# First loads cut and reordered, first layer norm in two parts of two tiles

## The reference, cut to what matters

```
x = x + attention0(layernorm(x))     # 3 heads, softmax over the first token axis, then mean over heads, fc
x = x + ffn0(layernorm(x))           # ternary-quantised weights
x = x + attention1(layernorm(x))     # 16 heads, causal
x = x + ffn1(layernorm(x))           # int8 product
layernorm(x) = (x - mean) / sqrt(var + 1e-5)
attention0: Q = x Wq[h].T, K = x Wk[h].T, V = x Wv[h].T
            scores = Q K.T / 16,  out = mean over h of softmax(scores) V,  then out @ fc_w.T + fc_b
```

## Time and profile before

| | us |
|---|---|
| median of three runs | 505.29 |
| the profiled execution | 505.88 |
| its span in the trace | 504.10 |
| PE busy | 482.8 (96%) |
| DVE busy | 378.2 (75%) |
| ACT busy | 295.4 (59%) |
| POOL busy | 282.5 (56%) |
| TensorE clock granted, mean | 0.991 |

### The profile page before, as it was taken

One profiled execution on the slowest core, in us unless ns is written; L12 is line 12 of the kernel. 1 busy time (PEld: TensorE's weight loads), 2 busy tenths in 40 slices (PEclk: granted clock), 3 DMA queues, 4 the chain that ended last, 5 costly groups with the idle time before them and its releaser, 6 DMA issues.

```text
span 504.1 us, 8912 instructions
## 1 busy us (share of the span) xinstructions
PE 482.8 (96%) x3020; PEld 429.8 (85%) x3020; DVE 378.2 (75%) x964; ACT 295.4 (59%) x694; POOL 282.5 (56%) x378
## 2 busy tenths in 40 slices
PE   8999999999999977899999999999999999999984
PEld 7888998899888856799888999899889989899972
DVE  2776776775746578788779888788878897667897
ACT  2355336535554645676667676667757766655663
POOL 1344244323665556786667786777767796511344
PEclk9999999999999999999999999999999999999996
DMA  9900000000010017564864764764765654100002
GB/s 278 380 22 2 1 0 1 0 1 1 24 42 1 0 46 184 159 187 109 213 182 127 195 181 114 210 179 122 202 178 149 177 170 131 36 1 1 0 2 83
DMA packets 54380, 51.58 MB, mean 102 GB/s; under 512 B 3520, under 2 KB 49728, under 8 KB 54336
## 3 DMA queue, kind: packets, MB, share of 16 engines
q1 hardware_dynamic: 53248, 49.98, 34.7%
q10 hardware_dynamic: 1088, 1.05, 0.6%
HBM read 32.92 MB, written 18.09 MB: 101 GB/s over the span
## 4 chain that ended last, share of the span: by engine, by line
PE 71%; DVE 13%; POOL 4%; issue 4%; DMA 3%; ACT 3%; SPq 1%; DVEq 0%; POOLq 0%; ACTq 0%
PE bank L405 19%; PE bank L407 18%; PE bank L406 18%; PE bank L700 3%; PE bank L698 3%; PE bank L699 3%; POOL HID_lo L1156 2%; DMA Wv_sb<-wv 2%; DVE BT L1535 2%; PE bank L628 1%; PE bank L627 1%; DVE SM L1516 1%; PE bank L709 1%; ACT E L906 1%; DMA turned_dram<-BT 1%
## 5 line engine op out<-in xcount | busy, mean ns | idle before, releaser
L1187 POOL TENSOR_TENSOR PT_lo<-MV,PT_hi 128x512 fp32r<-128x512 f32 (+1 forms) x104 | 91.5, 909 | 51.5 <-ACT PT_hi L998 51.1
L987 ACT ACTIVATE PR<-SM,nmax 128x128 f32<-128x128 f32 (+3 forms) x128 | 72.0, 563 | 62.6 <-DVE nmax L1516 62.1
L1132 POOL TENSOR_TENSOR E_lo<-E,E_hi 128x512 fp32r<-128x512 f32 x24 | 31.0, 1297 | 54.0 <-ACT E_hi L911 46.8
L1516 DVE CUSTOM_DVE_ANT_0 SM<-bank,causal 128x384 f32<-128x384 f32 (+3 forms) x102 | 54.0, 530 | 9.3 <-PE bank L700 6.4
L405 PE MATMUL bank<-XT_hi,W_hi 128*128 128x512 f32 x128 | 52.3, 409 | 5.2 <-DVE V_lo L1498 3.7
L998 ACT CAST PT_hi<-MV 128x512 fp32r<-128x512 f32 (+1 forms) x104 | 42.1, 453 | 19.6 <-DMA MV<-turned_dram 19.2
L1535 DVE STREAM_TRANSPOSE BT<-PR 128x128 f32<-128x128 f32 (+1 forms) x104 | 48.2, 492 | 5.6 <-POOL PR L1171 3.8
L407 PE MATMUL bank<-XT_hi,W_lo 128*128 128x512 f32 x128 | 50.5, 394 | 0.0
L406 PE MATMUL bank<-XT_lo,W_hi 128*128 128x512 f32 x128 | 50.2, 392 | 0.0
L406 PE MATMUL bank<-PT_lo,V_hi 128*128 128x128 f32 (+3 forms) x130 | 41.5, 319 | 0.0
L407 PE MATMUL bank<-PT_hi,V_lo 128*128 128x128 f32 (+3 forms) x130 | 41.5, 319 | 0.0
(11 more groups left out here) (189 smaller groups left out, 1602.6 us busy)
## 6 DMA issues: line engine op xcount, KB each, us to landing
MV<-turned_dram SPq DMA_DIRECT2D x104, 160.0 KB, 3.2
turned_dram<-BT SPq DMA_DIRECT2D x26, 384.0 KB, 2.9
stage<-pack SPq DMA_DIRECT2D x32, 256.0 KB, 3.9
turned_dram<-BT SPq DMA_DIRECT2D x26, 256.0 KB, 3.3
X<-x SPq DMA_DIRECT2D x2, 512.0 KB, 8.9
wraw<-wupT SPq DMA_DIRECT2D x1, 1024.0 KB, 9.6
wraw<-wgateT SPq DMA_DIRECT2D x1, 1024.0 KB, 11.5
wraw<-wdownT SPq DMA_DIRECT2D x1, 1024.0 KB, 13.7
```

The source lines that it names most:

```text
L987: act.activation(PR[:, c, 0:(c + 1) * P], SM[:, c % 2, 0:(c + 1) * P], ACT.Exp, bias=nmax1[:, c:c + 1], scale=-1.0, accum_out=sum1[:, c:c ...
L1132: pool.tensor_tensor(E0_lo[:, m, :], E0[:, m, :], E0_hi[:, m, :], ALU.subtract).then_inc(e0_lo, 1)
L1187: pool.tensor_tensor(by_quad(PT_lo[w % 2], c), moved_part(w, c), by_quad(PT_hi[w % 2], c), ALU.subtract).then_inc(mv_lo, 1)
L1516: dve.tensor_tensor_reduce(SM[:, c % 2, 0:n], s_bank(w, c)[:, 0:n], mask, 1.0, HIGHEST, ALU.add, ALU.min, nmax1[:, c:c + 1]).then_inc(s_ma ...
```

## The change

It does five things.

1. Wk and Wq of head 0 are loaded in two halves of 128 KB (128 rows each), each pair with a semaphore of its own (`ld_first`). Use 0 on PE goes over the half (d) outside and over the columns (e) inside, so that its first two products need the first halves only.
2. On SP, Wv of head 0 stands ahead of x; x of sequence 0 comes in two loads of two tiles (`ld_x0`). Wv of heads 1 and 2 goes to ACT's queue, behind fcT, which keeps its place.
3. The first statistics, the addition of epsilon and the power are done for tiles 0 and 1, then for tiles 2 and 3 (`first_var`, `first_rstd`), and normalising waits for each part by itself.
4. On PE, tiles 0 and 1 are transposed in front of the first half of use 5, tiles 2 and 3 in front of its second half.
5. `project_y` waits for XT_lo of one half of the columns at a time.

The diff, cut to its core:

```diff
         def _(sp):
-            for h in range(H0):
+            for k in range(KD):
+                sp.dma_start(Wk_sb[:, k, :], wk0[0][k * P:(k + 1) * P, :]).then_inc(ld_first[k], 16)
+            for h in range(1, H0):
                 sp.dma_start(Wk_sb[:, KD * h:KD * (h + 1), :],
                              wk0[h].rearrange("(k p) e -> p k e", p=P)).then_inc(ld_qk0[h], 16)
-            sp.dma_start(X[:, 0:CT, :], x[0].rearrange("(c p) d -> p c d", p=P)).then_inc(ld_x[0], 16)
-            for h in range(H0):
-                sp.dma_start(Wv_sb[:, KD * h:KD * (h + 1), :],
-                             wv0[h].rearrange("(k p) e -> p k e", p=P)).then_inc(ld_v0[h], 16)
+            sp.dma_start(Wv_sb[:, 0:KD, :], wv0[0].rearrange("(k p) e -> p k e", p=P)).then_inc(ld_v0[0], 16)
+            for i in range(2):
+                sp.dma_start(X[:, 2 * i:2 * i + 2, :], x[0][2 * i * P:2 * (i + 1) * P, :].rearrange(
+                    "(c p) d -> p c d", p=P)).then_inc(ld_x0[i], 16)
             sp.dma_start(X[:, CT:TILES, :], x[1].rearrange("(c p) d -> p c d", p=P)).then_inc(ld_x[1], 16)
...
             for g in range(GF_USES):
                 h = g % H0
+                dst = pj0_bank(g)
+                if g == 0:
+                    for d in range(KD):
+                        pe.wait_ge(ld_first[d], 32)
+                        for e in range(KD):
+                            mm = pe.matmul(dst[:, e * D:(e + 1) * D], Wq_sb[:, d, e * P:(e + 1) * P], Wk_sb[:, d, :],
+                                           start=(d == 0 and e == 0), stop=(d == KD - 1), skip_group_check=True)
+                    mm.then_inc(pj0_psum, 1)
+                    continue
...
-                if g == H0 + 2:
-                    pe.wait_ge(consts, 1)
-                    layernorm_turn(0)
...
                 for e in range(KD):
+                    if g == H0 + 2:
+                        pe.wait_ge(consts, 1)
+                        layernorm_turn(0, 2 * e, 2 * e + 2)
...
                 b, h = divmod(s, H0)
-                pe.wait_ge(xt_lo, 2 * (b + 1))
...
                     for k in range(KD):
+                        pe.wait_ge(xt_lo, 2 * b + k + 1)
...
         def _(act):
-            for h in range(H0):
+            for k in range(KD):
+                act.dma_start(Wq_sb[:, k, :], wq0[0][k * P:(k + 1) * P, :]).then_inc(ld_first[k], 16)
+            for h in range(1, H0):
...
             act.dma_start(fcT_sb[:], fcT.rearrange("(k p) o -> p k o", p=P)).then_inc(ld_fc, 16)
+            for h in range(1, H0):
+                act.dma_start(Wv_sb[:, KD * h:KD * (h + 1), :],
+                              wv0[h].rearrange("(k p) e -> p k e", p=P)).then_inc(ld_v0[h], 16)
...
-            rstd(0)
+            rstd(0, 0, 2)
+            pool.wait_ge(first_var, 1)
+            pool.tensor_tensor(ln_rs[:, 2:CT], ln_ve[:, 2:CT], neg_half[:, 2:CT], ALU.pow).then_inc(first_rstd, 1)
...
             for g in range(GF_USES):
+                if g == H0:
+                    for i in range(2):
+                        dve.wait_ge(ld_x0[i], 16)
+                        ln_statistics(0, 2 * i, 2 * i + 2)
+                        ln_variance(0, 2 * i, 2 * i + 2)
+                    ln_normalise(0, 0, 2)
+                    ln_normalise(0, 2, CT)
                 dve.wait_ge(pj0_hi, g + 1)
...
-                if g == H0 - 2:
-                    dve.wait_ge(ld_x[0], 16)
-                    ln_statistics(0)
-                    ln_variance(0)
-                if g == H0 - 1:
-                    ln_normalise(0)
```

More of the change, by code:

```diff
@@ L201, in build @@
         ld_qk0 = [sem(f"ld_qk0_{h}") for h in range(H0)]
+        ld_first = [sem(f"ld_first{k}") for k in range(KD)]
+        ld_x0 = [sem(f"ld_x0_{i}") for i in range(2)]
+        first_var, first_rstd = sem("first_var"), sem("first_rstd")
         ld_v0 = [sem(f"ld_v0_{h}") for h in range(H0)]
@@ L486, in _, with layernorm_turn @@
         def _(pe):
-            def layernorm_turn(k):
+            def layernorm_turn(k, c0=0, c1=CT):
                 b = k % 2
                 b0, b1 = LN_BANKS[k]
-                for c in range(CT):
+                for c in range(c0, c1):
                     pe.wait_ge(ln_norm, CT * k + c + 1)
@@ L494, in layernorm_turn @@
                         mm = pe.transpose(bank[bk][:, c * P:(c + 1) * P], XN[:, c, j * P:(j + 1) * P], ident[:])
-                mm.then_inc(xt_psum, 1)
+                if c1 == CT:
+                    mm.then_inc(xt_psum, 1)
             pe.wait_ge(warm_set, 1)
@@ L505, in _ @@
                 else:
+                    pe.wait_ge(ld_fc, 16)
                     pe.wait_ge(ld_v0[h], 16)
-                    pe.wait_ge(ld_fc, 16)
-                if g == H0 + 2:
-                    pe.wait_ge(consts, 1)
-                    layernorm_turn(0)
                 if g >= 3:
                     pe.wait_ge(pj0_done, g - 2)
-                dst = pj0_bank(g)
                 for e in range(KD):
+                    if g == H0 + 2:
+                        pe.wait_ge(consts, 1)
+                        layernorm_turn(0, 2 * e, 2 * e + 2)
                     for d in range(KD):
@@ L1238, in ln_variance @@
                 dve.wait_ge(ln_aggr, CT * k + c1)
-                dve.tensor_scalar(ln_ve[:, c0:c1], ln_mv[:, c0:c1, 1], EPS, None, ALU.add).then_inc(ln_var, 1)
+                dve.tensor_scalar(ln_ve[:, c0:c1], ln_mv[:, c0:c1, 1], EPS, None,
+                                  ALU.add).then_inc(first_var if k == 0 and c0 > 0 else ln_var, 1)
             def ln_normalise(k, c0=0, c1=CT, part=0):
                 b = k % 2
-                dve.wait_ge(ln_rstd, k + 1 + part)
+                if k == 0 and c0 > 0:
+                    dve.wait_ge(first_rstd, 1)
+                else:
+                    dve.wait_ge(ln_rstd, k + 1 + part)
                 for c in range(c0, c1):
```

## The result

The changed kernel took a median of 507.50 us (506.63 to 508.60, eight runs), the kernel before 505.25 in the same comparison (504.79 to 507.00, eight runs): ratio 1.0038 [1.0025, 1.0051], some 1.9 us slower. Forecast were 505.1 and a range that ended at 506.1. The profiled execution took 507.54, its span is 505.7; before 505.88 and 504.1.

A forecast was written before the change was run, and what follows sets the result against it. The prediction took the start, PE's loads and the layer norm arriving together, as the bound; of a 0.86 us lead 0.16 was left, 505.29 - 0.16, say 505.1 us, range 504.4 to 505.8, eight in ten 504.2 to 506.1.

The forecast's parts named there:

- When the loads land: Step on the first loads: landings counted from KB ahead on both queues; x's halves at 10.8 and 12.4 us.
- The other Wq and fcT keep their places: Loads behind head 0's halves: claimed to land as before, at 6.6, 8.2 and 10.0 us.
- Uses 1 and 2 run 6.65 to 10.37: PE at the start: use 3 follows without a gap, uses 3 and 4 end at 14.09 us instead of 14.95.
- PE is idle in the first slice only: Reading of the profile page's slices: what the change can reach lies in the first 22 us.
- ACT's first XT_hi is ready at 16.8, ahead of DVE: Ahead of `project_y`: DVE's XT_lo comes later, so `project_y` begins at 17.66 us instead of 17.82.
- The late x: Rival at the layer norm: x's second half lands late, at 14.43 costing +1.47 us, 506.8; chance 0.14.
- DVE and POOL: Rival in the second layer-norm round: the two engines hinder each other, +0.64 us, 505.9; chance 0.14.
- The surviving head start: Rival at the start: PE's whole lead of 0.86 us is kept, giving 504.4 us; chance 0.14.
- Carried to the end: Behind the first scores: nothing seen waits for a clock time, so the 0.16 us gain reaches the end.
- A time that moves by more than the start does: Sign that the forecast is wrong: it would mean something behind 22 us changed.
- 0.14 for slower: Chance that the whole kernel gets slower by more than 0.2%, 1.0 us; no change had 0.72.
- 16 engines need not drain two queues in step: Argument at the loads for x's second half landing late, where +1.47 us was claimed; chance 0.14.

The follow-up runs named there:

- after_whole_first: The changed kernel with Wk and Wq of head 0 loaded whole and use 0 in its old order; ratio to the kernel before 1.0001 [0.9982, 1.0020].
- before_order: The kernel before with only the loads reordered, x and first loads whole, layer norm in one part; one run, 507.70 us (kernel before: median 505.49).
- after_again: The changed kernel run once more, unedited; ratio to the kernel before 1.0027 [1.0011, 1.0044].
- before_delay: The kernel before with five unused products of 128 columns on PE ahead of the first `project_y`; ratio to the kernel before 1.0031 [1.0015, 1.0047].
- after_halves_wq_warm: The changed kernel with Wk of head 0 whole, only Wq halved, and eleven warming products for eight; ratio to the kernel before 1.0024 [1.0004, 1.0044].

## Why the prediction was wrong, point by point

**The step that failed** stands under "When the loads land": "The other Wq and fcT keep their places: 6.6, 8.2, 10.0." The working counted bytes on the queues, so cutting the first loads could change nothing for those behind them. In the changed kernel they landed at 7.55, 9.0 and 2.67 + 7.8 = 10.5; with both first loads cut, use 1 began at 7.56 to 9.22 in five of six executions (6.96 in the sixth) instead of 6.65; the 9.22 holds a late use 0 too. With the first loads whole the same count holds: in after_whole_first the first half of x landed at 2.7 + 8.1 = 10.8, as forecast; in before_order x at 12.4. The byte count was right where it had been read, and its use on loads of another size was not tested by any row. What the runs show in its place is 16 completions of a load that drift apart once both first loads are cut: over 1.6 to 2.9 us for fcT in five of six executions, 0.75 before. The reason for that is open.

**PE.** "Uses 1 and 2 run 6.65 to 10.37" became 7.56 to 11.12 with a second reason in that profile: use 0 at the lower clock, ending at 7.58. The forecast took 1.86 us a use, from the earlier trace rows, without asking at which level it would run 0.66 us earlier. after_again separates the two: full clock, and use 1 at 7.99. Right was that use 3 follows without a gap and that PE is then idle before the first transposition (0.65 us, forecast 0.3).

The forecast's first reading, "PE is idle in the first slice only", does not stand in the page: it gives PE eight tenths of that slice, warming products among them, and not the one tenth named ahead of the forecast, and seven tenths of some later slices. The sums do not use it.

**DVE.** Each duration held: 1.13 us from one round's statistics to the next, powers 0.73 and 0.79, XN 0.73 twice. GF_hi of use 2 was 0.92 late (11.32 for 10.40), and this was handed on: statistics 12.56 (11.66), second round 13.69 (12.82), second XN 15.83 (14.97).

**XT_lo and `project_y`.** "ACT's first XT_hi is ready at 16.8, ahead of DVE" was wrong by a little: DVE was idle for 0.25 us until XT_hi, in after_whole_first too. A slip in the forecast's own times lies behind it. It had the first XN at 13.81 and the second statistics from 12.82 to 14.06, both on DVE, whose stream has both rounds of statistics ahead of the first XN. In after_whole_first POOL's power was done at 13.84, and XN began at 14.07, when the second round ended: 0.23 us that the transpositions, half of use 5 and XT_hi hand on. Besides, 0.14 us of issue stand between XT_lo and `project_y`. This is why even without the halves the scores come 0.2 later than before, and not 0.16 earlier. `project_y` began at 18.85 instead of 17.66: 0.92 from GF_hi, 0.12 on the way to XT_lo, 0.15 behind it.

**The rivals.** The late x lost as the mechanism, although its 506.8 lies nearest to the result: the second half of x landed at 3.6 + 9.4 = 13.0, later than the 12.95 from which it was to cost, yet the second statistics began at 13.69, when ln_ve of the first two was under way (13.62 to 13.79), in turn and without a gap, not at the landing. DVE was itself late by then. The Trainium skill, "DMA: Bandwidth & Descriptors", section "Anatomy of one DMA", gives each DMA a fixed part of about 2.0 us, for another issue path than this kernel's. Paid in turn, that would by the prediction's estimate from that page have put x near 14.4; 13.0 was measured here, and 3.5 + 8.8 = 12.3 in after_whole_first. DVE and POOL did not hinder each other (0.73). The surviving head start was not seen in any kernel with the change's layer norm: with use 3 at 10.36, DVE's chain took it up, as argued.

**Carried to the end.** before_delay shows that a late start is not given back; one for one lies in its interval. The start lost 0.99 us in the one profile and 1.42 in the other; the runs lost 1.9 us (1.0038, 1.3 to 2.6) and 1.4 us (1.0027, 0.6 to 2.2). The second pair fits. In the first the start of the one profile lost less than the runs' interval, so the other executions lost more at the start, or something was added behind it; that stays open. "A time that moves by more than the start does" cannot be told from a profile here, since the rest of the span scatters by some 2 us on either side from one execution to the next.

**The chances.** 0.14 for slower was too little. The list of rivals had a late x, the load that was moved; it had no late Wq, a load that was to stay, and no clock. That "16 engines need not drain two queues in step" was written down for x alone.

## What to carry to other kernels

Cutting the first load of a queue to start earlier is not free for the loads behind it, and a count of bytes does not show the cost: read their landings in several traces of the cut kernel before counting on them. Where a start hangs on several landings, a gain at the first use is worth nothing until the second use is in time. Where the engine would stand idle between its warming products and the first real ones before the clock has risen, look at the length of the passes behind that gap: it tells the level. Longer warming took that gap away in after_halves_wq_warm; it did not help the kernel before (1.0005).

## What was not expected of the hardware

- Two loads of 128 KB at the head of both queues held back whole loads behind them by 0.9 to 2 us (use 1 at 7.56 to 8.65 where the cut was by rows, 6.65 by the byte count; one execution, 6.96, without it). The mean rate at 3.6 to 7 us was 230 to 303 GB/s in the three late executions shown, against 366 before. With one queue cut three executions show no wait for a late load of head 1 (scores 22.12, 21.97, 21.33); in three others, all with Wq cut, PE waited for Wq, 0.77 us ahead of use 0 or 0.69 and 0.62 us ahead of use 1. The cause of the long packets stays open, and one execution has them (30) without a late load.
- PE began its warming products at 0.97 or 0.98 each time, and the clock's rise came at 3.87 (before), 4.51 and 6.84 (two executions of the changed kernel, PE busy without a break up to the rise), and, with PE idle from 4.76 to 5.53, at 10.09. Passes of 634 ns became 380.
